# A hybrid layer on one core: convolution taps and the second cumulative sum read their operands in PSUM, norm constants move to ScalarE, all queues ordered anew

## What is computed

```python
def _layernorm(x, eps=1e-05):                       # eight half norms a sequence in the kernel
    return (x - mean(x)) / sqrt(var(x) + eps)

# mamba: xs, z = split(x @ W_in.T); 512 channels, causal convolution of 4 taps
xc = silu(conv1d(xs, conv_w, left_pad=3) + conv_b)
# ... dt, B, C from xc; h[t] = exp(dt*A) h[t-1] + dt*B*xc; y = (C . h + D*xc) * silu(z)

# wkv, 1024 channels
e  = exp(clip(-w * steps_left + K, -20, 10)); eu = exp(clip(U + K, -20, 10))
past_attention = cumsum(e * V, axis=1)              # the second cumulative sum
past_energy    = cumsum(e, axis=1)                  # the first
WKV = (shift(past_attention) + eu * V) / (shift(past_energy) + eu)
out = (sigmoid(R) * WKV) @ Wo.T + bo
```

## Time and profile before

| | us |
|---|---|
| median of three runs | 1877.59 |
| the profiled execution's own time | 1873.11 |
| its span | 1871.3 |
| first scan starts | 78.9 |
| last scan ends | 1633.6 |

### The profile page before, as it was taken

How to read it: one execution, slowest core, us unless ns; L and a number is a source line. 1 busy time by engine, 2 the same in 40 slices (tenths; PEclk the granted TensorE clock), 3 DMA queues, 4 the chain that set the end, 5 groups by cost and what they waited for, 6 DMA issues and landing times. The chain is left out here.

```text
span 1871.3 us, 18954 instructions
## 1 busy us (share of the span) xinstructions
PE 1489.6 (80%) x4800; PEld 720.6 (39%) x4800; DVE 1646.3 (88%) x2109; ACT 1178.2 (63%) x1705; POOL 1389.5 (74%) x1035
## 2 busy tenths in 40 slices
PE   4262358778879888989979798988989697988987
PEld 1120113333435335443535345443635253445454
DVE  3299899999999989999999999999999999994571
ACT  3674457676658765877567575876677356743621
POOL 0669997986997698886987679886988876761340
PEclk8685669899989889999989899999999898999999
DMA  7533434522434432452334434362335222211210
GB/s 230 213 120 107 157 118 154 188 94 92 146 101 160 149 121 90 128 190 96 117 115 156 137 96 137 118 211 87 113 109 172 90 80 94 94 55 49 62 40 29
DMA packets 167614, 225.20 MB, mean 120 GB/s; under 512 B 13457, under 2 KB 104082, under 8 KB 167506
## 3 DMA queue, kind: packets, MB, share of 16 engines
q1 hardware_dynamic: 167506, 223.99, 36.8%
HBM read 179.90 MB, written 39.85 MB: 117 GB/s over the span
## 5 line engine op out<-in xcount | busy, mean ns | idle before, releaser
L932 POOL TENSOR_TENSOR bu<-rep,bc 128x512 f32<-128x512 f32 x512 | 696.3, 1383 | 107.0 <-PE ps_y L1435 102.2
L1248 DVE TENSOR_TENSOR_SCAN ps_d<-ps_d,bu 128x512 f32<-128x512 f32 x384 | 458.1, 1212 | 59.7 <-POOL bu L932 50.3
L1076 ACT ACTIVATE ps_d<-rep,scale_a 128x512 f32<-128x512 f32 x512 | 337.9, 683 | 209.9 <-DVE bu L1255 186.6
L1384 PE MATMUL ps_r<-xT,wgu 128*128 128x512 f32 x768 | 360.0, 611 | 25.1 <-ACT kv L1113 6.6
L975 ACT ACT_TABLE_LOAD x191 | 245.1, 1283 | 76.5 <-PE ps_r L1384 29.7
L1384 PE MATMUL ps_r<-mix,wkv 128*128 128x512 f32 x512 | 254.4, 640 | 40.3 <-DVE mix L1316 16.2
L1255 DVE TENSOR_TENSOR bu<-ps_d,bc 128x512 f32<-128x512 f32 x384 | 252.3, 674 | 0.5
L1435 PE MATMUL ps_y<-bu,sel 128*32 128x512 f32 x1024 | 156.3, 686 | 118.9 <-DVE bu L1255 78.5
L1384 PEld LDWEIGHTS ps_r<-xT,wgu 128*128 128x128 f32 x768 | 144.2, 194 | 229.3 <-issue 220.5
L937 POOL TENSOR_TENSOR bu<-bu,bc 128x512 f32<-128x512 f32 x128 | 174.9, 1367 | 49.4 <-DVE bu L1248 48.8
L949 POOL TENSOR_TENSOR kv<-sums,kv 128x1024 f32<-128x1024 f32 x64 | 150.8, 2357 | 77.4 <-DVE sums L1345 45.3
(11 more groups left out here) (98 smaller groups left out, 2077.8 us busy)
## 6 DMA issues: line engine op xcount, KB each, us to landing
rep<-dd_scratch SPq DMA_DIRECT2D x128, 512.0 KB, 4.6
wgu<-gu_scratch SPq DMA_DIRECT2D x96, 256.0 KB, 2.7
bc<-bc_scratch SPq DMA_DIRECT2D x64, 256.0 KB, 3.6
dd_scratch<-xs SPq DMA_DIRECT2D x32, 512.0 KB, 3.4
wo<-w_o_dram SPq DMA_DIRECT2D x16, 512.0 KB, 3.9
win<-w_in_dram SPq DMA_DIRECT2D x64, 128.0 KB, 2.2
wr<-w_r_dram SPq DMA_DIRECT2D x64, 128.0 KB, 2.6
wkv<-w_k_dram SPq DMA_DIRECT2D x64, 128.0 KB, 2.3
```

Source lines behind the costliest of these rows:

```text
L932: pool.tensor_tensor(bu[:, i % BU, :], rep[:, g % REP, 1, :], bc[:, 0, q, :], ALU.mult)\
L1076: act.activation(ps_d[D_BANK[i]][:, :], rep[:, g % REP, 0, :], ACT.Exp, scale=scale_a[:, a, NQ * j + q:NQ * j + q + 1]).then_inc(decay_rea ...
L1248: dve.tensor_tensor_scan(states, d[:, :], bu[:, i % BU, :], 0.0, ALU.mult, ALU.add)\
L1384: last = pe.matmul(dst, lhs, rhs, start=n == 0, stop=n == len(pairs) - 1)
```

## The change

The two DVE instructions with an SBUF copy of a product as input read the product where it lies in PSUM. The copy to `xs` is gone, the taps read the bank of `p_in` and write the part of `xc` they reach; a bank of `p_in` is released by its third DVE tap. `v_ev` becomes two 128x512 instructions, of which the second writes e*V back into the bank of `p_v`, and `v_evsum` scans it there; the bank is released by the scan. `variance`, `norm` and `shifts` are gone; `deviation` on ACT makes the same from logarithm and exponential. All `ORDER` strings and `BANKS` are new.

```diff
-                "p_in": (xs_ready, i + 1) if i < JD else (sz_ready, i - JD + 1),
+                "p_in": (conv_tap, TAP_DONE[TAPS * i + TAPS - 1]) if i < JD else (sz_ready, i - JD + 1),
-                "p_v": (ev_ready, i + 1),
+                "p_v": (ev_summed, i + 1),
...
-            def norm(f, seq, i):
-                pool.wait_ge(n_var[f].sem, at(n_var[f], seq, i + 1))
-                pool.tensor_tensor(rstd[f][:, part], var_eps[f][:, part], minus_half[:, part], ALU.pow)
...
+            def deviation(f, seq, i):
+                part = slice(2 * (i % 2), 2 * (i % 2) + 2)
+                act.wait_ge(n_moments[f].sem, at(n_moments[f], seq, 2 * (i + 1)))
+                need("natural_log_exp_and_others")
+                act.activation(rstd[f][:, part], moments[f][:, part, 1], ACT.Ln, bias=eps[:, 0:1]).then_inc(n_log[f].sem, 1)
+                act.activation(minus_mean[f][:, part], moments[f][:, part, 0], ACT.Identity, scale=-1.0)\
+                    .then_inc(n_rstd[f].sem, 1)
+                act.wait_ge(n_log[f].sem, at(n_log[f], seq, i + 1))
+                act.activation(rstd[f][:, part], rstd[f][:, part], ACT.Exp, scale=-0.5).then_inc(n_rstd[f].sem, 1)
+                act.wait_ge(n_rstd[f].sem, at(n_rstd[f], seq, 2 * i + 2))
+                for t in range(2 * (i % 2), 2 * (i % 2) + 2):
+                    last = act.activation(shift[f][:, t:t + 1], minus_mean[f][:, t:t + 1], ACT.Identity,
+                                          scale=rstd[f][:, t:t + 1])
+                last.then_inc(n_shift[f].sem, 1)
...
-                            act.copy(xs[:, i, TAPS - 1:], src[:, :]).then_inc(xs_ready.sem, 1)
...
-                        act.wait_ge(xs_ready.sem, at(xs_ready, m, i + 1))
-                        act.activation(xc[:, i, :], xs[:, i, 0:T], ACT.Identity, bias=col("conv_b", i),
-                                       scale=col("conv_w", TAPS * i)).then_inc(first_tap.sem, 1)
+                        src = full(m_full, m, "p_in", i)
+                        act.activation(xc[:, i, :], src[:, :], ACT.Identity, bias=col("conv_b", i),
+                                       scale=col("conv_w", TAPS * i + TAPS - 1)).then_inc(first_tap.sem, 1)
...
-            def variance(f, seq, i):
-                dve.tensor_scalar(var_eps[f][:, part], moments[f][:, part, 1], EPS_LN, None, ALU.add)
-            def shifts(f, seq, i):
-                dve.scalar_tensor_tensor(shift[f][:, part], moments[f][:, part, 0], -1.0, rstd[f][:, part],
...
-                        dve.scalar_tensor_tensor(xc[:, j, :], xs[:, j, tap:tap + T], col("conv_w", i), xc[:, j, :],
+                        src = ps_r[BANK[m, "p_in", j]]
+                        dve.scalar_tensor_tensor(xc[:, j, back:], src[:, 0:T - back],
+                                                 col("conv_w", TAPS * j + TAPS - 1 - back), xc[:, j, back:],
                                                  ALU.mult, ALU.add).then_inc(conv_tap.sem, 1)
...
-                        dve.scalar_tensor_tensor(rows(i, "ev", "euv"), src[:, :].unsqueeze(1).to_broadcast([P, 2, T]),
-                                                 col("bv", i), rows(i, "e", "eu"), ALU.add, ALU.mult)\
-                            .then_inc(ev_ready.sem, 1)
+                        dve.scalar_tensor_tensor(kv[:, row(i, "euv"), :], src[:, :], col("bv", i), kv[:, row(i, "eu"), :],
+                                                 ALU.add, ALU.mult).then_inc(ev_ready.sem, 1)
+                        dve.scalar_tensor_tensor(src[:, :], src[:, :], col("bv", i), kv[:, row(i, "e"), :],
+                                                 ALU.add, ALU.mult).then_inc(ev_ready.sem, 1)
...
-                        dve.tensor_tensor_scan(sums[:, 1, 1:], ones[:, 0:1].to_broadcast([P, T]), kv[:, row(i, "ev"), :], 0.0,
+                        dve.tensor_tensor_scan(sums[:, 1, 1:], ones[:, 0:1].to_broadcast([P, T]),
+                                               ps_r[BANK[r, "p_v", i]][:, :], 0.0, ALU.mult, ALU.add)
```

More of the change, by code:

```diff
@@ L101 @@
     "p": (
[L102 to L126, removed]
@@ new lines @@
+        "p_v p_recept p_y p_recept p_k p_post*2 p_v p_dt p_k fp_turn p_v p_wo p_wo2 fp_turn2 fp_turn fp_turn2 "
+        "fp_gate fp_up fp_gate fp_up p_y fp_gate fp_up fp_gate fp_up p_wo p_y p_wo2 p_k p_y p_v fp_gate fp_up "
+        "fp_gate fp_up p_dt hp_turn fp_down p_y fp_down2 fp_down p_wo p_wo2 p_y fp_turn fp_down2 p_wo p_wo2 "
+        "rp_turn hp_turn p_y p_in fp_turn2 fp_turn fp_turn2 p_in*2 p_y rp_turn2 rp_turn rp_turn2 p_in*2 rp_gate "
+        "rp_up p_in p_xproj p_in p_y p_in rp_gate rp_up rp_gate p_y rp_up rp_gate rp_up rp_gate p_y rp_gate "
@@ L674, in hybrid_block @@
         clipped = signal("clipped", CT)
[L675 removed]
+        ev_ready = signal("ev_ready", 2 * CT, first=2 * CT)
         e_summed = signal("e_summed", CT)
@@ L992, in run @@
                     m = s = f = r = t
-                    if unit == "ha_norm":
+                    if unit == "ha_std":
+                        deviation("h", t, i)
+                    elif unit == "ha_norm":
                         normalize("h", m, i, xin, xin)
+                    elif unit == "fa_std":
+                        deviation("f", t, i)
                     elif unit == "fa_norm":
@@ L999, in run @@
                         normalize("f", f, i, xr, xnf)
+                    elif unit == "ra_std":
+                        deviation("r", t, i)
                     elif unit == "ra_norm":
@@ L1007, in run @@
                     elif unit == "a_in":
-                        src = full(m_full, m, "p_in", i)
-                        if i < JD:
-                            prev = before(m)
-                            if i == 0 and prev is not None:
-                                for k in range(2):
-                                    act.wait_ge(dd_stored[k].sem, at(dd_stored[k], prev, dd_stored[k].per))
-                            act.copy(xs[:, i, TAPS - 1:], src[:, :]).then_inc(xs_ready.sem, 1)
-                        else:
-                            j = i - JD
-                            if j >= 2:
-                                act.wait_ge(sz_stored[j % 2].sem, at(sz_stored[j % 2], m, 16))
-                            need("silu_and_others")
-                            act.activation(sz[:, j % 2, :], src[:, :], ACT.Silu).then_inc(sz_ready.sem, 1)
+                        src, j = full(m_full, m, "p_in", i), i - JD
+                        if j >= 2:
+                            act.wait_ge(sz_stored[j % 2].sem, at(sz_stored[j % 2], m, 16))
+                        need("silu_and_others")
+                        act.activation(sz[:, j % 2, :], src[:, :], ACT.Silu).then_inc(sz_ready.sem, 1)
                     elif unit == "a_tap":
@@ L1230, in run @@
                         aggregate("h", t, i)
-                    elif unit == "hv_eps":
-                        variance("h", t, i)
-                    elif unit == "hv_shift":
-                        shifts("h", m, i)
                     elif unit == "v_tap":
-                        j, tap = i // TAPS, i % TAPS
-                        if tap == 1:
+                        j, back = i // TAPS, i % TAPS
+                        src = ps_r[BANK[m, "p_in", j]]
+                        if back == 1:
                             dve.wait_ge(first_tap.sem, at(first_tap, m, j + 1))
```

599 lines of the change are left out of this document (291 added, 308 removed), and 114 rows, old and new, of tables (BANKS, ORDER).

## The result

The changed kernel takes 1804.39 us (median of four runs, 1802.19 to 1807.01) against 1877.59 for the kernel before; the ratio is 0.9613, 95% interval 0.9597 to 0.963, that is 73 us less. The forecast was 1797 within 1765 to 1850.

A forecast was written before the change was run, and what follows sets the result against it. The prediction took DVE, 96% busy in the middle stage, as the bound. Middle -82, head -1 and tail +2 us sum to -81, taking the median from 1877.6 to 1797 us, range 1765 to 1850.

The forecast's parts named there:

- work taken from DVE is worth its time in the middle: Middle stage, 80 to 1634 us: with DVE busy 96%, work removed from it shortens the run; little in the tail.
- Taps: DVE, middle: 84 taps taking 94.0 us drop to 741 ns each with a PSUM operand, a gain of 31.8 us.
- Second cumulative sum: DVE, middle: 50 scans taking 84.4 us drop to 1.212 us each with a PSUM operand, a gain of 23.8 us.
- `v_ev` in two: DVE, middle: one instruction of 1.272 us becomes two of 0.741, 50 times, a loss of 10.5 us.
- Variance and shifts: DVE, middle: 108 instructions on two columns go, 25.3 + 28.3 = 53.6 us gained.
- Collisions of what stays: DVE, middle: first cumulative sum and mixes meet a relieved POOL less; 9 us taken of at most 26.9.
- Idle time of DVE: DVE, middle: waits rise from 59 to 85 us, between no change and a doubled share (114 us).
- Deviation on ACT: ACT: logarithm, negation, exponential and two products, about 1.2 us each, 54 of them 65 us in the middle.
- "That is hidden.": ACT, middle: its 1140 us of work stay covered, as DVE still has 247 us more.
- PSUM does not free the taps: Rival on DVE: the new forms still wait for POOL, so the time is 1862; chance 0.03.
- The banks: Rival: PE waits for banks that DVE frees late, at most 144 us, about 1897 with 100; chance 0.05.
- The next bound: Rival, middle: 53 us from longer-held banks on PE, or from ACT's 93 added, reach DVE, giving 1850; chance 0.24.

The follow-up runs named there:

- the old order's run: Kernel before in its own order and banks, with only the norm's constants moved to ACT (variance, norm and shifts struck out): 1869.58 us, ratio 0.9968.
- run 14: Not a run number: in "the old order's run 14 of 49", 14 is microseconds of the 49 by which DVE's records fell; that run took 1869.58 us.
- less_dve_old: Kernel before without the last step of the reciprocal on DVE (64 instructions of 0.68 us), only signalled in its place: 1869.04 us, ratio 0.9963.
- act_more: Changed kernel with twelve more two-column activations on ACT in each deviation, 768 in all, results unread: 1848.78 us, ratio 0.985.
- norm_back: Changed kernel in its new order with variance and shifts back on DVE, the power on POOL and no deviation on ACT: 1860.55 us, ratio 0.9912.
- less_dve_new: Changed kernel without the last step of the reciprocal on DVE (64 instructions of 0.68 us), only signalled in its place: 1795.64 us, ratio 0.9569.

## Why the prediction was right, step by step

The forecast was right in the prices of the instructions and 7 us off in the time. One of its premises was not: that work taken from DVE is worth its time in the middle. Part of the closeness is luck. In spans the forecast was -81 and the result is -70 us, 11 off; the medians came nearer since the profiled execution of the kernel before stood 4.5 us under its median and that of the changed one only 1.0. And the 11 us are two errors that pull apart, DVE's work 9 us lower than predicted and its idle time 20 us higher. By its own steps:

- **Taps.** Predicted 31.8 us for 84 at 741 ns; they run at 734 and the line fell from 94.0 to 58.9, 35.1 us. Right.
- **Second cumulative sum.** Predicted 1.212 us each and 23.8 in all; measured 1.202 and 25.5, of which 1.2 are the one instruction fewer in the stage. Right.
- **`v_ev` in two.** Predicted a loss of 10.5; 35.9 + 36.6 against 63.6 is 8.9, and 10.5 if 50 are counted on both sides. Right, also for the one with input and output in the same bank (748 ns).
- **Variance and shifts.** Their lines are gone, 53.6 us, but that is not what DVE gains by it. A record of DVE begins some 0.08 us before the one ahead of it ends, and time in which two overlap counts once. DVE's timeline of the kernel before shows it (start, duration):

```profile
560.12 0.67 DVE L1218 TENSOR_TENSOR hf<-hf,ps_r 128x512 f32<-128x512 f32 x1
560.71 1.21 DVE L1248 TENSOR_TENSOR_SCAN bu<-ps_d,bu 128x512 f32<-128x512 f32 x1
561.84 0.65 DVE L1218 TENSOR_TENSOR hf<-hf,ps_r 128x512 f32<-128x512 f32 x1
```

  560.12 + 0.67 is 560.79, 0.08 past the next start, and 560.71 + 1.21 is 561.92. Summed over the middle the records of the kernel before make 1640.1 us and cover 1495.3; those of the changed one make 1514.0 and cover 1378.4. So 9 of the 126 us by which the records fell are no busy time, and in the old order's run 14 of 49.
- **Collisions of what stays.** I took 9 of at most 26.9 us. The first sum fell by 14.2 (1.3 of it the one instruction fewer), the mixes of L1316 by 6.0: 20.2 of the 26.9. This is the term that was too small, and it made good for the overlap: DVE's middle was predicted at 1387 us and is 1378.
- **Idle time of DVE.** Predicted 85 within 59 to 114, measured 105. This is the step that carries the error of the sum: middle predicted -82, measured -71. I had expected more waits because PE, ACT and the banks are nearer; the waits for PE grew by 29.7 us and those for ACT by 20.7.
- **Work taken from DVE is worth its time in the middle.** It held only together with the new strings, where 117 us less gave 71. With the strings left alone, DVE 96% busy and ACT untouched, 30.3 us less gave 2.1 us of the middle (`less_dve_old`). A share of 96% did not mean that DVE alone set the time.
- **Deviation on ACT.** Predicted 0.28 + 0.19 + 0.19 + 2 x 0.28, measured 0.289 + 0.187 + 0.203 + 2 x 0.287: 1.25 us, from lines through 256 and 512 columns and a pointer's 0.09 us. The Trainium skill's page "ScalarE: Activation LUTs", section "What ACT_TABLE_LOAD costs", has 186 ns and 0.833 ns a column with some 93 ns for each pointer; the trace agrees for the negation (187 ns) and within 10 ns for those with a pointer, and the exponential takes 15 ns more. ACT in the middle was predicted at 1140 us and is 1122: its records grew by 94 us, the 93 that I had added, and the time that they cover by 74.
- **"That is hidden."** Wrong as a statement on ACT. `act_more` shows that ACT's time costs 0.7 of what is added, and `norm_back` that the move pays all the same in the new order, 56 us. The sum came out near since the new strings were laid out with ACT's work in them; that its place and not ACT's idle share hides it is argued from this. For the move alone, in the old order, I expected 1823 to 1842 us, and the run gives 6 us.
- **Head and tail.** Predicted -1 and +2, measured +0.3 and +0.7; the 12 more table loads of the tail cost nothing that shows.
- **The rivals.** PSUM does not free the taps: refuted by their maximum of 751 ns. The banks: PE's waits behind L1316 and L1216 are some 19 us where those for the same banks were 26.5, and freeing the banks early moves DVE's idle time by 2 and 10 us; refuted in the size that I gave, 53 to 144. The next bound was the rival nearest to the truth: with idle time 20 us over my value the result lies 7 of the 53 us towards it. Of the signs that I had named only one fails, and narrowly: DVE is busy 92.9% of the middle and not over 93%.

The rule weighed against the taps, from the Trainium skill's page "VectorE: DVE Perf Modes", section "Rules for kernel authors", was to copy out of PSUM first where many operations follow. Here three taps follow, and reading PSUM directly costs nothing: 736 ns as the median against 747 with both inputs in SBUF. The 65 ns that the prediction estimated from that page's table are not in the trace. What decides is the other engine: every long tap began under a running POOL instruction. The Trainium skill's page "SBUF — State Buffer", section "Who interferes with whom", says that a DVE instruction with two SBUF inputs contends with a GpSimd instruction that reads SBUF, and the spreads and the counts above agree with it.

## What to carry to other kernels

Where DVE and POOL both work all the time, look at the spread of each DVE line and not at its mean. In this kernel the lines whose quickest instructions matched their PSUM twin and whose slowest took twice as long or more had two SBUF inputs, and moving one of them into PSUM took the whole excess away. Do not count such a gain, or any removed instruction, as time while the queues stay as they are: here 30 to 35 us taken from the busiest engine gave 6 or 7 in the old order, and 117 us gave 73 when all queues were laid out for it. And do not rank the parts of a finished change by undoing them one at a time, nor call an engine free because it is idle a quarter of the time: work added to any of the three engines cost time here.

## What was unexpected in the hardware

- A DVE instruction that writes back into the PSUM bank that it reads (L1303, 742/748/752 ns as minimum, median and maximum by its line) costs no more than one from PSUM to SBUF (L1301, 718/738/752).
- In the scan of L1316 the broadcast `ones` is still an SBUF input and only the data lie in PSUM. With this one SBUF input it is clear of POOL: 52 of its 64 began under a running POOL instruction, and the maximum is 1222 ns.
- With the collisions of taps and sums gone POOL gains more than its own powers cost it (40.5 us): its product for the scan fell from 1383 to 1295 ns on the mean, 47 us over 511 of them, with the median of 1271 unchanged. The prediction had this gain without a number.
- Records of neighbouring DVE instructions overlap by 0.08 us, so a group of many short instructions looks dearer than it is. In `less_dve_new` 49 instructions of 0.68 us, 33 us, are missing from the middle and DVE's busy time there fell by 22.3; 7 of the 11 us between are this overlap.
